# Decoder block on one core: the experts' units in another order, stacks stored in one run, second group's rows loaded earlier

## What is computed

```python
# x (4, 1024, 256), context (4, 154, 256); 16 heads of 16; 8 experts, hidden 512
x = layernorm(x + self_attention(x))      # latent projections of 128, rotary part added to q and k
x = layernorm(x + cross_attention(x, ctx, mask))
def ffn(x, choice_w, w1, w2):             # experts choose their tokens
    k = S * 2 // E                        # 256 tokens for each expert and batch
    probs = softmax(einsum('bsd,ed->bse', x, choice_w))
    G, I = top_k(swapaxes(probs, -1, -2), k)
    x_in = take_along_axis(x[:, None], I[..., None], axis=2)
    h = silu(einsum('bekd,edf->bekf', x_in, w1))
    x_mlp = einsum('bekf,efd->bekd', h, w2)
    return zeros_like(x).at[b_idx, I].add(G[..., None] * x_mlp)
x = layernorm(x + ffn(x))
```

## Time and profile before

| | us |
|---|---|
| median of 3 runs | 1686.72 (1682.87 to 1689.72) |
| the profiled execution | 1685.06 |
| its span | 1683.3 |
| mean granted clock of PE | 0.965 |

### The profile page before, as it was taken

How to read it: one execution, slowest core, us unless ns; L and a number is a source line. 1 busy time by engine, 2 the same in 40 slices (tenths; PEclk the granted TensorE clock), 3 DMA queues, 4 the chain that set the end, 5 groups by cost and what they waited for, 6 DMA issues and landing times. The chain is left out here.

```text
span 1683.3 us, 24438 instructions
## 1 busy us (share of the span) xinstructions
PE 1530.9 (91%) x8366; PEld 702.9 (42%) x8366; DVE 1230.8 (73%) x2543; ACT 864.3 (51%) x1626; POOL 438.4 (26%) x559
## 2 busy tenths in 40 slices
PE   7889999898999898989998989899987888999996
PEld 3322324424222244343232442423224436888875
DVE  5778854887888868978888689788885765664445
ACT  3367784343777743547777434477773341111111
POOL 6330001601300016013000160130000213666764
PEclk9799999999999999999999999999997898999998
DMA  6410000454100005541000054500000124555595
GB/s 178 120 55 1 2 30 9 145 116 126 40 2 1 30 5 147 117 126 39 2 1 30 10 155 104 149 16 2 2 1 26 52 70 129 113 113 110 105 267 142
DMA packets 110360, 121.52 MB, mean 72 GB/s; under 512 B 20700, under 2 KB 91868, under 8 KB 110236
## 3 DMA queue, kind: packets, MB, share of 16 engines
q1 hardware_dynamic: 95516, 99.74, 20.7%
q0 software_dynamic: 13728, 18.89, 6.2%
q10 hardware_dynamic: 992, 1.32, 0.2%
HBM read 68.76 MB, written 31.09 MB: 59 GB/s over the span
## 5 line engine op out<-in xcount | busy, mean ns | idle before, releaser
L1245 ACT ACTIVATE pT<-banks 128x512 f32<-128x512 f32 x1184 | 650.2, 600 | 277.4 <-PE banks L2121 156.2
L1565 DVE TENSOR_REDUCE nmf<-banks 128x1 f32<-128x1024 f32 x512 | 601.2, 1219 | 104.9 <-PE banks L2036 104.2
L2121 PE MATMUL banks<-qst,kst 99*128 99x512 bf16 x1024 | 342.8, 385 | 12.9 <-DVE nmf L1565 6.3
L2036 PE MATMUL banks<-kst,qst 96*128 96x512 bf16 x1024 | 311.1, 386 | 7.8 <-DVE nmf L1565 4.0
L2153 PE MATMUL banks<-pT,V 128*32 128x512 f32 x2048 | 274.6, 608 | 16.7 <-ACT oT L1233 12.3
L2121 PEld LDWEIGHTS banks<-qst,kst 99*128 99x128 bf16 x1024 | 95.7, 97 | 289.2 <-ACT pT L1245 185.1
L957 POOL CAST nmp<-nmf 128x16 bf16<-128x16 f32 x64 | 12.6, 197 | 727.0 <-issue 593.8
L2036 PEld LDWEIGHTS banks<-kst,qst 96*128 96x128 bf16 x1024 | 96.3, 99 | 121.5 <-DVE nmf L1565 26.5
L1415 ACT ACTIVATE kst<-banks 128x512 f32<-128x512 f32 x64 | 38.1, 598 | 206.7 <-PE banks L2481 206.7
L1011 POOL DMA_INDIRECT acc_rows<-kst,tok_s x62 | 100.1, 1614 | 41.4 <-issue 17.1
L1825 DVE TENSOR_SCALAR kst<-banks,gate 128x256 f32<-128x256 f32 x64 | 28.0, 479 | 93.1 <-PE banks L2494 93.1
(11 more groups left out here) (255 smaller groups left out, 2105.2 us busy)
## 6 DMA issues: line engine op xcount, KB each, us to landing
qst<-q_parts SPq DMA_DIRECT2D x36, 256.0 KB, 4.9
kst<-k_parts SPq DMA_DIRECT2D x36, 256.0 KB, 7.7
qst<-in_w SPq DMA_DIRECT2D x16, 512.0 KB, 5.2
qxs<-in_w SPq DMA_DIRECT2D x16, 512.0 KB, 5.4
qxs<-oT SPq DMA_DIRECT2D x48, 128.0 KB, 2.5
qst<-oT SPq DMA_DIRECT2D x48, 128.0 KB, 2.5
xb<-in_x SPq DMA_DIRECT2D x4, 1024.0 KB, 6.7
x_rows<-z SPq DMA_DIRECT2D x4, 1024.0 KB, 8.8
```

Of the source, the lines that this page charges most:

```text
L1245: act.activation(pT[:, n % RING_P, :], PS[:, banks[what, n], :], ACT.Exp, scale=scale).then_inc(s_ex, 1)
L1565: dve.tensor_reduce(nmf[:, m % 2, j, t:t + 1], scores.rearrange("p a n -> p (a n)"), AX.X, ALU.max, negate=True).then_inc(s_smu, 1)
L2036: ins = pe.matmul(pair[:, half, :], qst[0:KQ, h, t * P:(t + 1) * P], kst[0:KQ, h, half * N:(half + 1) * N], start=True, stop=True)
L2121: ins = pe.matmul(ps, kst[0:KM, head, kc * P:(kc + 1) * P], qst[0:KM, head, cols], start=True, stop=True)
```

## The change

Three things are changed.

1. `self_attention(0)` no longer loads the rows of group 1: that load now stands before `load_context(0)` in SP's stream.
2. The rows of the stacks have another order. In the first batch chunk c fills rows 48 c to 48 c + 47 (`dims_of`), where the chunks alternated. In DRAM the rows stand as (half of the heads, dimension, head of the half), so that what one stack load reads is one contiguous piece of 256 KB. q and k are changed alike.
3. Units 0 to 22 are as before. Unit 28 is expert 7 of the third batch, which was unit 23; units 23 to 27 are experts 0 to 4 of the last batch, 29, 30 and 31 its experts 5, 6 and 7. The last unit uses the weights that unit 28 loaded. The sums of the third batch are loaded behind the outputs of the second, directly before those of the last batch; its statistics stand at unit 30 and its layer norm at unit 31.

```diff
--- before.py
+++ after.py
@@ -201,6 +201,7 @@
 
 TURN_SELF, TURN_CROSS = 3, 4
 START = 2
+MC = 2
 BY_SYNC, BY_POOL = 3, 9
 LATE_HEADS = 4 * (BY_SYNC + BY_POOL)
 BITS = 30
@@ -209,6 +210,7 @@
 TURNS = BITS // AT_ONCE
 COLS = 5
 FINAL_FROM = 26
+FINAL_AT = {26: 0, 27: 1, 30: 2}
 EARLY = B - 1
 UNITS = B * E
 LAST = UNITS - 1
@@ -219,9 +221,17 @@
 PICK_BANK = 1
 
 
+LAST_FROM, LENT_TURN = EARLY * E - 1, 28
+EXPERT_OF = list(range(E)) + [0, 1, 2, 3, 4, 7, 5, 6]
+
+
 def unit(n):
 
-    return (n // EARLY, n % EARLY) if n < EARLY * E else (n - EARLY * E, B - 1)
+    if n < LAST_FROM:
+        return n // EARLY, n % EARLY
+    if n == LENT_TURN:
+        return E - 1, EARLY - 1
+    return n - LAST_FROM - (n > LENT_TURN), B - 1
 
 
 def column(n):
@@ -231,7 +241,7 @@
 
 def weights_of(n):
 
-    return n // EARLY if n < EARLY * E else E + n - EARLY * E
+    return n // EARLY if n < LAST_FROM else E + n - LAST_FROM if n < LAST else weights_of(LENT_TURN)
 
 
 def last_unit(w):
@@ -601,6 +611,9 @@
         def parts_of(piece):
             return [part_x[:, k, :] if piece[1] == 8 else parts_at[SLOT[piece]][:, k, :] for k in range(3)]
 
+        def dims_of(c, t):
+            return slice(c * KQ // C + t, (c + 1) * KQ // C, len(TERMS))
+
         at_once = [s_item, s_evd, s_eva, s_evp]
         from_one = [s_xb, s_mask, s_p2, s_x2, s_nt, s_ne, s_gt, s_y, s_si, s_te, s_ye,
                     s_pk, s_pe2, s_pwx] + s_pw + s_nl
@@ -660,8 +673,7 @@
                 stack, which = (kst, 1) if name == "k" else (qst, 0)
                 for t, term in enumerate(TERMS):
                     if term[which] == part:
-                        sp.dma_start(stack[c * len(TERMS) + t:KQ:C * len(TERMS), late * 8:(late + 1) * 8,
-                                           half * N:(half + 1) * N],
+                        sp.dma_start(stack[dims_of(c, t), late * 8:(late + 1) * 8, half * N:(half + 1) * N],
                                      first_parts[2 * j + c][late:P:2, part, :]).then_inc(s, 16)
 
             def load_first(j):
@@ -701,14 +713,14 @@
 
             def rows_of(parts, c, half):
 
-                rows = parts.rearrange("k (d c h) n -> k c d h n", c=C, h=H)
+                rows = parts.rearrange("k (m c r) n -> k c r m n", m=MC, c=C)
                 return [rows[k, c, :, :, half * N:(half + 1) * N] for k in range(3)]
 
             def load_stack(dst, parts, mc, which, s, terms=range(len(TERMS))):
 
                 for t in terms:
                     term = TERMS[t]
-                    src = parts[term[which], :, :].rearrange("(d i m) n -> m d i n", d=HD, m=2)[mc]
+                    src = parts[term[which], :, :].rearrange("(m d i) n -> m d i n", m=MC, d=HD)[mc]
                     sp.dma_start(dst[t:KQ:len(TERMS), :, :], src).then_inc(s, 16)
 
             def load_minus_max(b, n, rows):
@@ -737,11 +749,11 @@
                         sp.dma_start(kxst[t:KQ:len(TERMS), c * 8:(c + 1) * 8, 0:SK], src).then_inc(s_kx, 16)
 
             def self_attention(b):
-                for g in range(1, NG):
+                for g in range(1 if b else 2, NG):
                     load_minus_max(b, g, qst[:, g * G:(g + 1) * G, :])
 
             def load_expert(w):
-                e, i = w % E, w % WEIGHTS
+                e, i = EXPERT_OF[w], w % WEIGHTS
                 sp.dma_start(we1[i], a["w1"][e:e + 1, :, :].rearrange("a (c p) f -> p (a c) f", p=P)
                              ).then_inc(s_we[i], 16)
                 sp.dma_start(we2[i], a["w2"][e:e + 1, :, :].rearrange("a (c p) d -> p (a c) d", p=P)
@@ -852,6 +864,7 @@
             for dst, src in ((wo[:, :, :], chunks("Wo")), (w0[:, :, :], chunks("W0T")),
                              (w3[:, :, :], chunks("W3T")), (wch[:, :, :], chunks("choiceT"))):
                 sp.dma_start(dst, src).then_inc(s_w, 16)
+            load_minus_max(0, 1, qst[:, G:2 * G, :])
             load_context(0)
             self_attention(0)
             for b in range(B - 1):
@@ -877,11 +890,12 @@
                 wait_apart(sp, s_y, last_unit(w - WEIGHTS) + 1 + START)
                 load_expert(w)
                 if w == E + WEIGHTS:
-                    for b in range(EARLY):
+                    for b in range(EARLY - 1):
                         load_sum(b)
             for b in range(B):
-                if b == B - 1:
-                    load_sum(b)
+                if b == EARLY - 1:
+                    load_sum(EARLY - 1)
+                    load_sum(EARLY)
                 for half, done in enumerate((s_fv, s_fl) if b < EARLY else (s_fl, s_fv)):
                     tiles = slice(half * T // 2, (half + 1) * T // 2)
                     sp.wait_ge(done, b + 1)
@@ -1000,7 +1014,7 @@
                 q, k = divmod(n, SLOTS)
                 for j in range(2):
                     pool.indirect_dma_start(xg[k][:, j, :], None,
-                                            x2_rows[0:(EARLY if n < EARLY * E else B) * S, :],
+                                            x2_rows[0:(EARLY if n < LAST_FROM else B) * S, :],
                                             bass.IndirectOffsetOnAxis(tok_g[q % 2][:, k, j:j + 1], 0)
                                             ).then_inc(s_g[k], 16)
 
@@ -1052,7 +1066,7 @@
                         pool.wait_ge(s_evp, FIRST_AT.taken("P", FIRST_AT.nth(name, 4 * half + 2 + c) + 1))
                     for t, term in enumerate(TERMS):
                         if term[which] == part:
-                            pool.dma_start(stack[c * len(TERMS) + t:KQ:C * len(TERMS), 0:8, half * N:(half + 1) * N],
+                            pool.dma_start(stack[dims_of(c, t), 0:8, half * N:(half + 1) * N],
                                            first_parts[2 * j + c][0:P:2, part, :]).then_inc(s[half], 16)
 
             def bias_context(b):
@@ -1096,7 +1110,7 @@
 
             def gather_next(n):
 
-                if n == EARLY * E:
+                if n == LAST_FROM:
                     pool.wait_ge(s_x2, B * 32 + START)
                 wait_apart(pool, s_tk, n // SLOTS * 2 + 1, s_gt, n - SLOTS + 1 + START)
                 gather(n)
@@ -1114,8 +1128,8 @@
                 if n == SPREAD_FROM - 4:
                     pool.iota(tokens, pattern=[[1, S]], base=EARLY * S, channel_multiplier=0,
                               allow_small_or_imprecise_dtypes=True).then_inc(s_io, 1)
-                if FINAL_FROM <= n < FINAL_FROM + EARLY:
-                    last_rsqrt(n - FINAL_FROM)
+                if n in FINAL_AT:
+                    last_rsqrt(FINAL_AT[n])
             for half in range(2):
                 last_rsqrt_half(half)
 
@@ -1909,10 +1923,10 @@
                     scatter_tokens(q + 1)
                     if (q + 2) * SLOTS < UNITS:
                         take_choice(q + 2)
-                if FINAL_FROM < n <= FINAL_FROM + EARLY:
-                    apply_layernorm(n - FINAL_FROM - 1)
-                if FINAL_FROM <= n < FINAL_FROM + EARLY:
-                    last_statistics(n - FINAL_FROM)
+                if n - 1 in FINAL_AT:
+                    apply_layernorm(FINAL_AT[n - 1])
+                if n in FINAL_AT:
+                    last_statistics(FINAL_AT[n])
                 if SPREAD_FROM <= n < SPREAD_FROM + 2:
                     spread_rows(n - SPREAD_FROM)
             add_last(0)
```

## The result

| | kernel before | changed kernel |
|---|---|---|
| median of the timed runs | 1685.97 us (1682.87 to 1689.72, 5 runs) | 1678.94 us (1676.37 to 1679.76, 5 runs) |
| profiled execution, time / span | 1685.06 / 1683.3 us | 1678.94 / 1677.1 us |
| mean granted clock of it | 0.965 | 0.962 |

The ratio of the changed kernel to the one before is 0.9942, 95% interval 0.9914 to 0.9969. The medians lie 7.0 us apart, the ratio says 9.8 us of 1686; the forecast was a gain of 11.8 us and 1675.0 us. The change made the kernel faster by about half a per cent. The median is 3.9 us above the forecast: inside the range that was stated, and 0.9 us outside the forecast's own 1672 to 1678.

A forecast was written before the change was run, and what follows sets the result against it. TensorE, 91% busy, bounds the kernel through idle and low-clock stretches, then the scatter chain at the end. Gains 7.0 + 1.5 + 3.3 = 11.8 us take 1685.06 to 1673.3; with the median 1.7 higher, 1675.0 us, range 1666.0 to 1681.0.

The forecast's parts named there:

- rival (b): Tail: DVE's gating of unit 31 waits for the third batch's sums, the 3.3 us go, 1678.3 us; chance 0.15.
- Edit 1, 7.0 forecast: First self-attention: earlier row load removes PE's 4.38 us stop and the low clock behind it; 7.0 us, bounds 4.4 and 7.2.
- Edit 2, 1.5 forecast: Cross attention: contiguous stack loads gain a little, 1.5 us for three batches, bounds 8 and +1.
- the two waits: Cross scores (L2124): PE waits 5.3 us in all for ACT's nmT copy, held behind the stack loads.
- packet size was not what held the stack loads: Cross attention: stack loads ran at 230 GB/s, smaller-packet weight loads at 362, so only 1.5 us was taken.
- The first batch's new rows, 0 ± 1.4 forecast: PE's first score waits 2.71 us for its stacks; same DMAs and queues, so 0, half that wait either way.
- Edit 3, 3.3 forecast: Tail: new unit order starts the last batch's sum load and adds 3.3 us earlier; bounds 6 and 0.
- The forecast's first step: Scatter chain at the end: scatter 29 starts when its output is gated, 1651.7 instead of 1654.47, 2.8 us earlier.
- about 1 us: PE's new wait for gathered rows at 1608 us, where the moved weight and sum loads go.
- (a): Cross attention: contiguous source makes stack loads much faster, both nmT waits go, 8 instead of 1.5 us, 1668.5; chance 0.19.
- (c): First self-attention: the stop moves, the row load still lands late, only 1 to 2 us return, 1680.5; chance 0.09.
- (d): Cross attention: contiguous 16 KB pieces move at half the present rate, +29 us, about 1703; chance 0.07.

The follow-up runs named there:

- the one kernel meant to tell it: Changed kernel with the stores to q_parts and k_parts named with an outermost dimension of 8 instead of 64: 1683.53 us beside 1692.64, one run each.
- the kernel with both repairs: Changed kernel with the first batch's stacks in the old rows and DVE's second spread block ahead of the third batch's statistics: 1676.23 us, ratio 0.9928.

## Why the prediction was right, and where its sum was wrong

The direction and the range were right. The sum, 11.8 us, was 3.9 too large against the median's move from 1686.7, and 2.0 too large against the ratio. That it came so near is in part luck: one term was four times too small, one was 3.3 us for nothing, and they stand on opposite sides. The measured 1678.9 lies nearer to rival (b)'s 1678.3 than to the forecast's 1675.0.

- **Edit 1, 7.0 forecast.** The mechanism came as told, row by row: the load ahead of the stores, no wait, clock 1.00, and 6.8 us within the frames. The step that failed is what follows: the sum took every later frame at its old length and named nothing as late next, and DVE's maxima were (0.70 us of wait at 107.93, 1.1 us in all). Net 5.6 us, between the bounds; alone the edit had 5.9 us at the first scatter of its trace, which one trace can't price, and over its runs 2.5 us by the ratio (0.15% of 1687) and 4.3 at equal clock. That `kxst` and the stores behind it cost nothing was right: the next row load went at 117.05, long after their 106.1.
- **Edit 2, 1.5 forecast.** Mis-sized. Where the two waits stood, in batches 0 and 2, it gave 4.1 and 2.0 us, 6.1 in all; with the 1.6 of batch 1, which may be clock, it is 7.7, just under the far bound of 8. The step that failed was the inference from the rate: "packet size was not what held the stack loads", so little was taken. The rate indeed did not change, 241 and 240 GB/s. But PE's wait hung on when the loads begin and how fast they get going, 1.2 us and 38 GB/s better, and on a landing 2.0 us shorter; PE's waits of 3.1 us and less were short enough to be closed by that. I had weighed the stores on 16 engines as tenths of a us. The sooner start must come from the stores, since it lies ahead of the loads; whether from their 16 engines or from the new order of their rows was not settled, since the one kernel meant to tell it left the engines as they were. That 16 destination partitions hold the rate near 240 GB/s was argued in the prediction, and no run varied them.
- **The first batch's new rows, 0 ± 1.4 forecast.** They cost 1.5 us at the first score, just beyond the bound, and about 1 us behind it. "I take 0" had no row for it but that the DMAs are the same. They are, and their bytes too; which part of the writes is slower no run shows.
- **Edit 3, 3.3 forecast.** Nothing, so rival (b) has the right size. Its mechanism, DVE held by the third batch's sums, did not come: DVE gated unit 31 at 1655.77 as soon as PE had it, and PE's last sums wait 1.06 us for that at 1656.80, as they did before. The forecast's first step, 2.8 us at scatter 29, came as 1.8. It let the scatter start when the output is gated; that gating was only 0.1 us later than forecast, counted from unit 22's scatter, and 0.8 us passed between its end (1645.34) and the scatter (1646.16), for DVE's copy of the token numbers and POOL's start. The sum put nothing for them. What failed then was that the landings of the earlier trace rows were carried over to a place with another surrounding. Moving the third sum load put it beside scatter 29 (5.4 us). The statistics that wait for it put DVE's spread block onto the issue of scatter 30 (5.1 us). Moving the other two put them onto the gather of unit 27 (2.93 us where I had written "about 1 us"). The experiments show the first: without the load it is 4.6, and over all traces 4.4 to 4.7 without a load beside it, 4.9 to 6.5 with one. They show the third: with the loads later that wait is 0.85, though PE then waits at unit 31. Of the second they show 0.3 us; the block's being away came with 4.2, but one kernel has the block and 4.3.
- **The clock.** Not in the sum at all beyond edit 1. In this pair of traces six places cost the changed kernel 6.4 us. That is why the profiled executions are only 6.1 us apart, though edits 1 and 2 brought 5.6 and up to 7.7. It is not a steady price of the change: executions of the same kernel differ in it by as much, and over their runs the changed kernel's mean clock (0.963) is no lower than before's (0.962).
- **The rivals.** (a) had a part of the truth: the nmT waits went, but by 2 us less of landing, not by a much faster stream. (c) fell with the row at 94.45. (d) fell with 197 and 240 GB/s: the 16 KB pieces are not slow. (Its 29 us on 1675.0 make 1704, where 1703 is written.)

What stays open: which property of edit 2's stores brings the loads forward, what shortens the row load's landing beyond 0.6 us, why eight rows at every 6th land later than at every 12th, where 0.6 us of scatter 30's landing come from, and whether the kernel with both repairs beats the changed one. Its ratio is lower, 0.9928 against 0.9942, but the intervals overlap.
